# Per-batch copies of modulation and mask columns replaced by reads in place, in a four-layer sequence kernel on one Trainium2 core

## The reference

```python
# layer 0: layernorm, scale and shift, two state-space scans (forward, backward), gated; x + gate * out
# layer 1: layernorm, h * (1 + scale) + shift, permuted tokens, convolution, one state-space scan, gated
# a scan, for each token t, 512 channels e, 16 states n:
h = dA_t * h + dBu_t
y = jnp.einsum('ben,bn->be', h, C_t)
# layer 2: attention with 16 heads
att = att + (1.0 - mask) * -1000000.0
att = jax.nn.softmax(att, axis=2)
v = ((xn @ v_w + v_b) * src_mask[:, :, None]).reshape(Bx, Tx, H, -1)
h = layer_norm(y, sb_norm_w, sb_norm_b) * (1.0 + scale) + shift
h = jax.nn.silu(h) @ out_w + out_b            # x + h
# layer 3: linear attention with 8 heads
k = xn @ Wk + bk + (1.0 - src_mask) * -1000000.0
q = jax.nn.softmax(q.reshape(b, t, h, dh), axis=-1)
k = jax.nn.softmax(k.reshape(b, t, h, dh), axis=1)
v = ((xn @ Wv + bv) * src_mask).reshape(b, t, h, dh)
hh = _ln(y, ln2_w, ln2_b) * (1.0 + scale) + shift
```

## Time and profile before

| what | value |
|---|---|
| device time, three runs | 3707.52 us median (3702.73 to 3718.88) |
| span of the profiled execution (its own time is not given beside it) | 3709.0 us |
| instructions | 64650, of them 3590 on DVE |
| scans (L678) | 1536, 1211 ns each |
| products with C on POOL (L693) | 1536, 1287 ns each |
| granted clock of TensorE | 0.951 in the mean, 1.00 in most of the steady part |

### The profile page before, as it was taken

One profiled execution on the slowest core, in us unless ns is written; L12 is line 12 of the kernel. 1 busy time (PEld: TensorE's weight loads), 2 busy tenths in 40 slices (PEclk: granted clock), 3 DMA queues, 4 the chain that ended last, 5 costly groups with the idle time before them and its releaser, 6 DMA issues.

```text
span 3709.0 us, 64650 instructions
## 1 busy us (share of the span) xinstructions
PE 3242.9 (87%) x22078; PEld 2674.0 (72%) x22078; DVE 2851.3 (77%) x3590; ACT 2921.7 (79%) x6624; POOL 2833.8 (76%) x3087
## 2 busy tenths in 40 slices
PE   6677788899999999999999999899989999897876
PEld 2556667787777878787877778787877777675643
DVE  1568778889797979798887979798888979793621
ACT  1658878888889898888888898988988898873522
POOL 0578989888898889888888888888888889780500
PEclk8899999999999999999999999999999999997866
DMA  4112222222122222212221222212221222220100
GB/s 170 59 51 82 80 66 65 85 65 88 61 87 63 83 63 80 74 59 89 65 87 58 82 69 79 71 60 89 63 88 60 87 61 78 60 69 19 44 2 10
DMA packets 140951, 257.08 MB, mean 69 GB/s; under 512 B 15921, under 2 KB 33329, under 8 KB 140225
## 3 DMA queue, kind: packets, MB, share of 16 engines
q1 hardware_dynamic: 140626, 252.95, 22.0%
HBM read 233.16 MB, written 5.05 MB: 64 GB/s over the span
## 4 chain that ended last, share of the span: by engine, by line
PE 48%; ACT 22%; DVE 11%; POOL 6%; issue 6%; DMA 0%; SPq 0%; POOLq 0%; DVEq 0%; ACTq 0%
PE ps_b L574 10%; PE ps_y L602 9%; ACT decay L639 8%; POOL g L693 5%; DVE hst L678 4%; PE ps_x L771 4%; ACT dbut L649 4%; PE ps_x L1276 3%; PE ps_x L765 3%; PE ps_v L765 3%; PE ps_x L1301 2%; PE ps_v L771 2%; PE ps_x L774 2%; PE ps_v L790 2%; ACT pT L1355 2%
## 5 line engine op out<-in xcount | busy, mean ns | idle before, releaser
L693 POOL TENSOR_TENSOR g<-hst,c_bc 128x512 f32<-128x512 f32 x1536 | 1976.1, 1287 | 482.2 <-PE ps_y L602 349.0
L678 DVE TENSOR_TENSOR_SCAN hst<-decay,ps_b 128x512 f32<-128x512 f32 x1536 | 1832.7, 1211 | 399.0 <-PE ps_b L574 231.8
L639 ACT ACTIVATE decay<-delta,acoef 128x256 f32<-128x256 f32 x3072 | 1378.4, 498 | 56.8 <-DVE hst L678 56.4
L574 PE MATMUL ps_b<-ident,dbut 128*128 128x128 f32 x6144 | 951.9, 278 | 241.4 <-DVE hst L678 110.3
L658 POOL TENSOR_TENSOR dbut<-dut,bcm 128x256 f32<-128x256 f32 x1536 | 972.4, 633 | 190.7 <-ACT dut L864 190.7
L602 PE MATMUL ps_y<-ident,g 128*128 128x128 f32 x6144 | 943.0, 276 | 20.8 <-ACT u L965 17.4
L574 PEld LDWEIGHTS ps_b<-ident,dbut 128*128 128x128 f32 x6144 | 708.0, 143 | 333.3 <-ACT dbut L649 165.1
L602 PEld LDWEIGHTS ps_y<-ident,g 128*128 128x128 f32 x6144 | 734.6, 142 | 147.4 <-issue 55.5
L649 ACT ACTIVATE dbut<-dut,bcm 128x256 f32<-128x256 f32 x1536 | 767.4, 500 | 22.0 <-PE ps_b L574 18.8
L1355 ACT ACTIVATE pT<-ps_x 128x1024 f32<-128x1024 f32 x128 | 129.5, 1012 | 74.5 <-PE ps_x L1311 64.3
L1301 PE MATMUL ps_x<-qT,kT 18*128 18x256 f32 x1024 | 159.6, 433 | 16.7 <-ACT pT L1355 15.6
(11 more groups left out here) (192 smaller groups left out, 4080.3 us busy)
## 6 DMA issues: line engine op xcount, KB each, us to landing
c_bc<-c_rows SPq DMA_DIRECT2D x768, 256.0 KB, 3.2
rows_bc<-mod_rows SPq DMA_DIRECT2D x16, 384.0 KB, 4.4
ada_w<-in_ada_w_dram SPq DMA_DIRECT2D x1, 5120.0 KB
weights<-in_weights_dram SPq DMA_DIRECT2D x1, 4832.0 KB, 34.8
x<-in_x_dram SPq DMA_DIRECT2D x16, 256.0 KB, 3.8
x0p<-x SPq DMA_DIRECT2D x16, 256.0 KB, 2.3
xr<-x SPq DMA_DIRECT2D x16, 256.0 KB, 2.3
x<-x SPq DMA_DIRECT2D x16, 256.0 KB, 3.6
```

The lines of the kernel that those rows point to most:

```text
L574: last = nc.tensor.matmul(ps_b[:, u % 2, e * T + t * P:e * T + (t + 1) * P], dbut[:, u % NDBU, t, e * P:(e + 1) * P], ident[:, :], is_tran ...
L639: last = nc.scalar.activation(decay[:, u % (DA_AHEAD + 2), e, :], delta[s][:, eb, :], ACT.Exp, scale=acoef[:, s, eb, n:n + 1])
L678: nc.vector.tensor_tensor_scan(line(hst[:, u % NHST, :, :].rearrange("p e t -> p (e t)")), line(decay[:, u % (DA_AHEAD + 2), :, :].rearran ...
L693: nc.gpsimd.tensor_tensor(g[:, u % NG, :, :], hst[:, u % NHST, :, :], c_bc[:, k % NCB * CHUNK + n % CHUNK, :].unsqueeze(1) .broadcast_to([ ...
```

## The change

ACT reads scales and shifts in `mod_cols` and the mask columns in `CO` directly, by the batch's number. The five small tensors and their copies go, with the semaphore `cols_now`. The prologue loads both masks (16 rows each), turns them into (mask - 1) x 1e6 with one DVE instruction and stores them to memory as `mask_rows`; the main stage loads rows from there. Of `keymask`, now cleared once by POOL in the prologue, only the partitions 16, 48, 80 and 112 are loaded. DVE waits for the loads where the rows are used: at the keys of layer 2 and of layer 3. The maximum of the keys is negated by the reduction itself.

```diff
     "l2a": {
-        "DVE": (46, 49, 55, 55, 61, 63, 65, 70, 72, 74, 81, 83, 88, 95, 97),
+        "DVE": (46, 49, 55, 61, 63, 65, 70, 72, 74, 81, 83, 88, 95, 97),
...
+        mask_rows = nc.dram_tensor("mask_rows", (2, B, T), F32, kind="Internal").ap()
...
+            masks = sbp("masks", [2 * B, T])
...
                     for dst, src in rest:
                         sp.dma_start(dst, src).then_inc(S["loaded_rest"], 16)
+                    sp.dma_start(masks[0:B, :], dram["mask2"]).then_inc(S["masks_in"], 16)
+                    sp.dma_start(masks[B:2 * B, :], dram["mask3"]).then_inc(S["masks_in"], 16)
                     sp.dma_start(W[:, early:WTOT], dram["weights"][:, early:WTOT]).then_inc(stage_sems["weights_in"], 16)

                     sp.wait_ge(S["rows_ready"], 1)
                     sp.dma_start(mod_rows, rows[:, 0:4, :].rearrange("b r d -> b (r d)")).then_inc(S["rows_stored"], 16)
+                    sp.wait_ge(S["masks_ready"], 1)
+                    sp.dma_start(mask_rows.rearrange("l b t -> (l b) t"), masks[:, :]).then_inc(S["masks_stored"], 16)
                     sp.wait_ge(S["rows_stored"], 16)
+                    sp.wait_ge(S["masks_stored"], 16)
...
+                    done(pool.memset(keymask[:, :], 0.0))
...
                     done(nc.vector.tensor_copy(itok[:, :], itok_i[:, :]))
+                    dve.wait_ge(S["masks_in"], 32)
+                    nc.vector.tensor_scalar(masks[:, :], masks[:, :], 1.0, NEG, ALU.subtract, ALU.mult).then_inc(S["masks_ready"], 1)
...
         def l1_in_vector(dve, ch, b, at):
-            nc.vector.tensor_copy(cols1[:, :].unsqueeze(2), mod_cols[:, 0:2 * DB, bass.ds(b, 1)]).then_inc(S["cols_now"], 1)
             norm_stats(ch, b, "b", x1)
...
-            act.wait_ge(S["cols_now"], nth("cols_now", b, 1))
             act.wait_ge(S["xt_full_b"], nth("xt_full_b", b, 1))
             for d in range(DB):
-                last = nc.scalar.activation(xt_a[:, d, :], pair[:, d, :], ACT.Identity, scale=cols1[:, d:d + 1],
-                                            bias=cols1[:, DB + d:DB + d + 1])
+                last = nc.scalar.activation(xt_a[:, d, :], pair[:, d, :], ACT.Identity, scale=mod_cols[:, d, b:b + 1],
+                                            bias=mod_cols[:, DB + d, b:b + 1])
...
                 last = nc.scalar.activation(xt[:, d, :], bank(psum, k0, DB)[:, d, :], ACT.Silu,
-                                            scale=cols[:, d:d + 1], bias=cols[:, DB + d:DB + d + 1])
+                                            scale=mod_cols[:, q0 + d, b:b + 1], bias=mod_cols[:, q0 + DB + d, b:b + 1])
...
         def l2a_sync(sp, b, at):
-            sp.dma_start(keymask[:, :], dram["mask2"][bass.ds(b, 1), :].rearrange("b d -> (b d)")
-                         .partition_broadcast(P)).then_inc(S["key_in"], 16)
+            sp.dma_start(keymask[DH2:P:LANE, :], mask_rows[0, b, :].partition_broadcast(P // LANE)).then_inc(S["key_in"], 16)
...
-                                            ACT.Copy, scale=mask2[:, t:t + 1])
+                                            ACT.Copy, scale=c["mask2"][:, b * TB + t:b * TB + t + 1])
...
         def l2a_vector(dve, ch, b, at):
-            ch.done(nc.vector.tensor_copy(mask2[:, :], c["mask2"][:, bass.ds(b * TB, TB)]))
...
-            yield next(at)
-            dve.wait_ge(S["key_in"], nth("key_in", b, 16))
-            ch.done(nc.vector.tensor_scalar(keymask[:, :], keymask[:, :], 1.0, c["keyrow"][:, 0:1], ALU.subtract, ALU.mult))
             for k in range(2):
                 yield next(at)
+                if k == 0:
+                    dve.wait_ge(S["key_in"], nth("key_in", b, 16))
...
         def l2_tail_vector(dve, ch, b, at):
-            ch.done(nc.vector.tensor_copy(cols2[:, :].unsqueeze(2), mod_cols[:, 2 * DB:4 * DB, bass.ds(b, 1)]))
...
-            sp.dma_start(maskrow[:, :], dram["mask3"][bass.ds(b, 1), :].rearrange("b d -> (b d)")
-                         .partition_broadcast(P)).then_inc(S["mask_in"], 16)
+            sp.dma_start(maskrow[:, :], mask_rows[1, b, :].partition_broadcast(P)).then_inc(S["mask_in"], 16)
...
-                last = nc.scalar.activation(v3[:, t, :], bank(ps_x, 2, TB)[:, t, :], ACT.Copy, scale=mask3[:, t:t + 1])
+                last = nc.scalar.activation(v3[:, t, :], bank(ps_x, 2, TB)[:, t, :], ACT.Copy, scale=c["mask3"][:, b * TB + t:b * TB + t + 1])
...
         def l3_vector(dve, ch, b, at):
-            dve.wait_ge(S["mask_in"], nth("mask_in", b, 16))
-            ch.done(nc.vector.tensor_copy(mask3[:, :], c["mask3"][:, bass.ds(b * TB, TB)]))
-            ch.done(nc.vector.tensor_copy(cols3[:, :].unsqueeze(2), mod_cols[:, 4 * DB:6 * DB, bass.ds(b, 1)]))
-            ch.done(nc.vector.tensor_scalar(maskrow[:, :], maskrow[:, :], 1.0, NEG, ALU.subtract, ALU.mult))
             norm_stats(ch, b, "d", x3)
...
+            dve.wait_ge(S["mask_in"], nth("mask_in", b, 16))
             dve.wait_ge(S["k_full"], nth("k_full", b, 1))
...
-            ch.done(nc.vector.tensor_reduce(kmax[:, 0, :], k3[:, :, :], AX.X, ALU.max))
-            nc.vector.tensor_scalar(kmax[:, 1, :], kmax[:, 0, :], -1.0, None, ALU.mult).then_inc(S["k_sub"], 1)
+            nc.vector.tensor_reduce(kmax[:, 1, :], k3[:, :, :], AX.X, ALU.max, negate=True).then_inc(S["k_sub"], 1)
```

More of the change, by code:

```diff
@@ L47 @@
                convw=EB * CT, convb=EB, l2w=DB, l2b=DB, bq2=4, bk2=4, l3w=DB, l3b=DB, bk3=DB,
-               mask2=B * TB, mask3=B * TB, keyrow=1, onerow=1)
+               mask2=B * TB, mask3=B * TB, onerow=1)
 BIASROWS = ["bf", "bv2", "bo2", "bq3", "bv3", "bo3"]
@@ L78 @@
 FIRST = """
-loaded_ada loaded_fold loaded_rest consts cond_act ada_full ada_taken rows_ready rows_stored cols_full cols_taken alog_exp alog_done
+loaded_ada loaded_fold loaded_rest consts cond_act ada_full ada_taken rows_ready rows_stored cols_full cols_taken alog_exp alog_done masks_in masks_ready masks_stored
 fold_full fold_taken foldb_full foldb_done gather_ready dve_chain pool_chain
@@ L88 @@
 dt_read_2 du_ready_2 dut_full_2 dut_sb_2 ud_done_2 prep_done_2 c_stored_2 x_in row_in xn_a x0_done xt_full_a
-xt_sb_a z_full z_sb mx_full mx_sb mx_silu kept yb_full_0 yg_0 o_full_0 res_0 xr_in cols_now xn_b xt_full_b xt_sb_b
+xt_sb_a z_full z_sb mx_full mx_sb mx_silu kept yb_full_0 yg_0 o_full_0 res_0 xr_in  xn_b xt_full_b xt_sb_b
 xm_full xm_sb gz_full gz_sb conv_done conv_silu gate_in yb_full_1 yg_1 o_full_1 o_sb_1 og_full_1 res_1 key_in
@@ L214, in build @@
         blockmask = sb("blockmask", [P, P])
+        keymask = sb("keymask", [P, T])
         ps_b = ps("ps_b", [P, 2, 512])
@@ L449, in build @@
         dbc = [dbc_b, dbc_b, dbc_a]
-        cols1 = sb("cols1", [P, 2 * DB])
-        cols2 = sb("cols2", [P, 2 * DB])
-        cols3 = sb("cols3", [P, 2 * DB])
-        mask2 = sb("mask2", [P, TB])
-        mask3 = sb("mask3", [P, TB])
         st = sb("stats", [P, len(NORMS), TB, 6])
@@ L465, in build @@
         yv = sb("yv", [P, TB, D])
-        keymask = sb("keymask", [P, T])
         maskrow = gate1
@@ L1214, in tail_tensor, with tail_scalar @@
             pe.wait_ge(S[f"res_{n}"], nth(f"res_{n}", b, 1))
-        def tail_scalar(act, b, psum, k0, xt, cols, n, at):
+        def tail_scalar(act, b, psum, k0, xt, q0, n, at):
             if n == 2:
@@ L1640, in _ @@
                     "l2a": lambda b, at: l2a_scalar(act, b, at), "l2b": lambda b, at: l2b_scalar(act, b, at),
-                    "l2_tail": lambda b, at: tail_scalar(act, b, ps_x, 0, xt_x, cols2, 2, at),
+                    "l2_tail": lambda b, at: tail_scalar(act, b, ps_x, 0, xt_x, 2 * DB, 2, at),
                     "l3": lambda b, at: l3_scalar(act, b, at),
-                    "l3_tail": lambda b, at: tail_scalar(act, b, ps_x, 2, xt_a, cols3, 3, at)}))
+                    "l3_tail": lambda b, at: tail_scalar(act, b, ps_x, 2, xt_a, 4 * DB, 3, at)}))
             @block.vector
@@ L1712, in pack @@
               mask2=column(f["mask_BxS_ff1"].reshape(-1)), mask3=column(f["mask_BxSx1_fk1"].reshape(-1)),
-              keyrow=(NEG * key_row[:P])[:, None], onerow=one_row[:, None])
+              onerow=one_row[:, None])
     return {
```

## The result

The changed kernel takes **3680.9 us** (median of 10 runs, 3661.4 to 3700.1), the kernel before 3705.0 beside it: a ratio of 0.9935, 95% interval 0.9911 to 0.9960, or 24 us less. The profiled execution has a time of 3661.4, the fastest of the ten, and a span of 3659.7; in every run where both are given the span is 1.7 to 1.8 us under the time.

The account below looks back on a forecast made before the run. PE was taken as the bound in most of a period, so DVE time counts only where PE idles for it. Terms sum to 31.85 us, 20.2 steady and 11.6 outside: 3707.5 - 31.9, say 3676 (chance 0.48); own range 3665 to 3690, whole 3640 to 3703.

Parts of the forecast that it names:

- the 127 instructions: Sign of being right: DVE has 127 instructions less and is busy some 105 us less.
- The wait behind L1058, 18.2 us: Layer 1 column copy: removing it saves PE's whole 1.40 us wait in 13 periods, 18.2 us; bounds 0 to 23.
- the wait only moves: Rival, 0.20: the scaling of the same norm behind L1058 takes on the removed wait; 18.2 us lost, 3694.
- two scans stand between: Argument against the moved wait: two scans separate L1058 from the next scaling, and POOL's next work waits for them.
- Batch 1, 3.75: Layer 1 column copy in batch 1: it takes 4.14 us and PE waits 3.75, counted as 3.75 more gained.
- L1410, 4.5: Layer 2 column copy: nothing in the steady part, 3.9 us once in batch 12, 0.6 in the last three batches.
- Head of layer 3, 4.4: Three instructions L1520 to L1522: 2.0 us (12 x 0.17), 1.7 in batch 12, 0.7 in batch 15.
- "Nothing" for L1364, L1371, L1541: Mask columns, key mask, negation: no steady gain, as PE has no gap there; 0.4 in batch 13, 0.6 in tail.
- Its waits behind 1868 stay: Sign of being right: PE's waits around the layer 3 tail, 3.08 us idle of 11, remain.
- a stall elsewhere goes too: Rival, 0.12: held layer 3 tail scalings may pass POOL after the shift, 12 x 3.08 = 37 us more, 3639.
- DVE's time is all gained: Rival, 0.08: L1058's 1.79 and layer 3 head's 2.4 us come off whole, 4.2 x 12 = 50, giving 3646.
- The offset: Page span 3709.0 against run median 3707.5, 1.5 apart: taken as nothing, gains subtracted from the median.

Follow-up runs that it names:

- the kernel with the reduction: Changed kernel with layer 3 tail norm in PSUM, the two scalings of layer 0's second norm replaced by a copying reduction (mean and factor left out): 3610.9 us.

## Why the prediction was right, and where it was not

The forecast of 3676 met 3681 and 3672, and that is luck in part. The largest term of its sum, 18.2 of 31.9 us, was wrong by its mechanism and measured 4.4; time that the sum didn't have made up for it.

Of the signs that it named for itself, the 127 instructions and the end of the 1.40 us wait came true, and PE's wait for L1222's result went from 1.99 to 1.81. But DVE is busy 79 us less and not 105, the idle time behind 1868 did not stay where the hold is missing, and all three signs of a wrong mechanism came: the scaling behind L1058 is longer (1.15 to 1.81 us), a steady period without the hold is 0.7 us shorter and not at least 1, and PE's idle time moved to a place that was not named, the second norm of layer 0.

- **The wait behind L1058, 18.2 us: failed.** The observation was right (the 1.40 us is gone in every period), the step "I take the whole 1.40" was not. The rival "the wait only moves" held, and the sum's own lower bound for this term, 0, was near. I had the wait absorbed by the scaling of the same norm; that pair did grow, by 0.66 us, but PE's wait appeared behind the norm after, whose pair went from 1.03 to 2.11. Net: 0.37 us a period (201.29 to 200.92), 12 x 0.37 = 4.4 us. My argument against the rival, "two scans stand between", is refuted: the scans don't take up the wait (their mean stays at 1.211 us), and DVE's gain is carried past them to the next scalings, which take it up.
- **Batch 1, 3.75: mostly right.** 3.74 became 0.81.
- **L1410, 4.5: about right in size, 3.2 by the medians,** but with 0.14 us in each steady period, where I had nothing, and with a 3.9 that comes by chance: of six traces with this copy, one had it held twice, two once and three never.
- **Head of layer 3, 4.4: about right in all.** 2.5 by the medians; but by the trace 0.38 a period, where 0.17 was taken from PE's own gap.
- **"Nothing" for L1364, L1371, L1541: fits the steady part, not tested by itself.** Put back one at a time, the others cost 0.37, 0.14 and 0.38 us a period, 0.89 together, and the whole change is worth only 0.72 (201.64 to 200.92). Nothing is left for these three.
- **What the sum doesn't explain.** Between the traces of the two kernels with the norm in PSUM lie 22.7 us: 2.2 ahead of the first of the 12 starts, 9.5 in the eleven periods, 11.0 behind the last. The last figure is not accounted for: among the six traces of the changed kernel and its variants with the norm in PSUM this stretch alone differs by 7 us (566.6 to 573.5), and there is one such trace of the kernel before (584.5).
- **"Its waits behind 1868 stay": failed.** The rival "a stall elsewhere goes too" came true in part: 3 and 6 holds against 10 and 7. Its worth is not shown. By the ratios the change is worth 24 and 33 us with the hold possible and 25 without it (19 by the medians), so what the rarer hold adds lies between nothing and some 14 us. That the hold costs time was shown (some 60 us when it can't occur); that the change makes it rarer was not.
- **"DVE's time is all gained", 4.2 us a period: out.** The period fell by 0.72.
- **Two readings.** The offset was taken as nothing against a trace of 3709.0; the span lies 1.7 under the time, so that execution took about 3711, above the median of 3705, and it had 10 holds. And a period of that trace is 205.7 us in the mean, not about 207; nothing in the sum hangs on it.

## What to carry to other kernels

When an instruction that another engine holds up is removed, its wait can pass to the next one of the kind that is held, over instructions that aren't: here 1.74 of 1.79 us passed to two later pairs of scalings. Follow the engine's stream to those before counting a gain. Where an instruction sometimes takes 0.8 us and sometimes 4.4 at the same place, don't trust its count in one trace, and remove the cause instead of shifting the phase: moving one norm's source to PSUM was worth some 60 us, against 24 and 33 for eight instructions removed. And measure small parts on the version without the hold, where the runs of a kernel lie within 5 to 18 us instead of up to 43, beside the kernel that they are compared with and in the same set of runs. The version that beats both kernels is the change with this norm in PSUM, at 3623.8; the scaling with a step of two does not improve on it beyond the noise.

## What the hardware showed that I had not expected

The scaling of the layer 3 tail norm starts 0.01 to 0.07 us ahead of a POOL instruction at 80 of the 84 starts counted in the seven traces. 47 of these 80 end after 4.40 to 4.45 us and 33 after 0.81 to 0.83, and nothing that I found in the records before them tells which. (At the other four POOL had started 0.3 us earlier, and the scaling took 0.47.) When held, it is held through five POOL instructions in a row (three of 0.63 to 0.64, two of 1.29 to 1.30), not through one. It is no even draw everywhere: the next two starts behind the twelve were held in all seven traces, 14 of 14. What decides stays open.

PE's clock seems to take back part of a gain. In the kernel with the reduction, the same 12 us of two periods, with the same 8.98 us of PE's time and the same wait of 1.81 us for ACT in them (columns: window, us, PE, PEld, DVE, ACT, POOL busy, granted clock, DMA share, GB/s):

```profile
1752.00:1764.00 12.00, 8.98 (x59) 7.61 (x58) 9.67 (x17) 11.91 (x27) 7.58 (x9) 1.00 0.18 60
2152.00:2164.00 12.00, 8.98 (x44) 7.06 (x42) 8.28 (x15) 11.36 (x25) 7.22 (x8) 0.86 0.19 56
```

In the second the clock stood at half, 1.2 instead of 2.4 GHz, for a part of it, right behind waits of PE of 1.21 and 1.81 us; the first has the same two waits and kept the full clock, so they alone don't decide it. Such a fall comes in 7 of the 11 steady periods of that trace and in 1 of the changed kernel's with the norm in PSUM; those seven have 201.2 to 201.8 us, the four without a fall 199.55 to 200.33. From 835.25 to 3044.63 the eleven take 2209.4 us against 2214.9 there: 5.5 us less, where 11 x 1.2 = 13 would be gained if none had a fall. The other 5.3 of the 10.8 us between the two traces lie ahead of the first start and behind the last. Why the falls are more frequent here is not shown.
